# TensorE's signals in the gather stages move from the last matmul to a drain behind it

## The chip, the cores and the metric

One Trainium2 chip, of which the program uses one core. The metric is the device time of one execution in microseconds; lower is better. The engines are TensorE (PE: matmuls, and PEld: its weight loads), VectorE (DVE), ScalarE (ACT), GpSimd (POOL) and SyncE (SP). Each runs its own stream of instructions, and they wait for each other on semaphores.

## The reference

A graph network of two layers, and a mixture of six small experts behind it, on 12,500 nodes of 256 features and 200,000 edges plus a loop at each node:

```python
def gcn_conv(x, W, b, src, dst, n_nodes):
    ...
    norm = dinv[s] * dinv[d]                      # 1/sqrt(degree) of both ends
    xw = x @ W
    msg = xw[s] * norm[:, None]
    out = jax.ops.segment_sum(msg, d, num_segments=n_nodes)
    return out + b
...
out = jax.nn.relu(batch_norm(gcn_conv(x, W1, b1, ...), gamma1, beta1))
out = batch_norm(gcn_conv(out, W2, b2, ...), gamma2, beta2)
out = jax.nn.relu(out + identity)
...
x = x + gnn(layernorm(x), edges, ...)
x = x + experts(layernorm(x), ...)                # router, the best two of six experts
```

The edges arrive sorted by their target node `dst`. All is float32.

## The kernel before, in words

The kernel scales the rows by the degree first, sums the rows of each node's neighbours, and multiplies by W afterwards. It first builds tables of the edges (windows, indices, degrees), then writes the scaled rows to DRAM (`t_dram[0]`), runs a gather stage for layer 1, writes rows again (`t_dram[1]`), runs a gather stage for layer 2, and ends with the router (rows are scattered to `routed`) and the expert tiles.

A gather stage (`gathers` on GpSimd, `aggregate` on the others) works on `NG` = 208 groups of 1024 edges. A group is `CPG` = 8 gathers of 128 rows of 1 KB:

- GpSimd, line 678, fetches 128 rows of DRAM into one of 32 slots of `spare` with an indirect DMA. There is room for `RING` = 4 groups. Ahead of the first gather of group g it waits for `groups_used` >= g - 3, that is until TensorE has used the group four before it. Its indices come from ScalarE (line 801, `stage_ready`), which waits for `groups_used` too.
- VectorE makes a one-hot matrix for each 128 edges (line 1194, `oh_fast`): which of 128 nodes of a window the edge goes to. For group g + 2 it waits for `groups_used` of group g.
- TensorE, `fast`: eight matmuls of a one-hot tile with a slot (line 1753) sum the group into one PSUM bank. A float32 matmul leaves two records in the trace, so a group has 16. The last one raises `groups_used`. Then `turn_window` transposes the window of the group before it (`turn`, line 1653), the last transpose raising `win_turned`.
- ScalarE, line 810, copies the sums of a group out of PSUM to `win_rows` behind `groups_used`, and raises `win_kept`, for which `turn_window` waits.
- VectorE, line 1205, adds the turned window to `acc` behind `win_turned`, at a position that it reads from a table, and raises `ev_fast`.

Once in eight groups the linear part of a finished chunk of nodes lies between (`lin_begin`, `lin_finish`, line 1775 on TensorE; `scale`, line 1242, and `stats`, line 1248, on VectorE; `add_bias`, line 822, on ScalarE); `scale` raises `lin_scaled`. When all groups are added, VectorE raises `agg_done` (line 1266) and the last chunks of the linear part follow. Loops over the groups are hardware loops (`strides`), and the order on each engine is that of the program text.

Behind the second gather stage GpSimd makes masks for the router (lines 695 to 713) once `agg_done` is 2; VectorE reads them behind `masks_made` (lines 1361 to 1365). The masks lie in `spare` and `tables`.

Of the kernel before, what the change touches and what calls it, by code (L numbers as in the profile page):

```python
# [17 lines left out]
P = 128  # L18
# [4 lines left out]
CPG = 8  # L23
GE = EC * CPG
WIN = 128
# [52 lines left out]
def gnn_moe(nc, N, E, x, src, dst, W1, b1, W2, b2, gamma1, beta1, gamma2, beta2,  # L78
            rw1, rb1, rw2, rb2, ew1, eb1, ew2, eb2, ew3, eb3, out):
    D = x.shape[1]  # L80
    KH = D // P
    NX = ew1.shape[0]
    NCH, NG, NT, STRIDE = sizes(N, E)
# [45 lines left out]
    with ExitStack() as ctx:  # L129
# [42 lines left out]
        win_rows = sb("win_rows", [WIN, 2, D])  # L172
        ps = ctx.enter_context(nc.psum_tensor("ps", [P, 8, 512], F32))
# [36 lines left out]
        slots = spare[:, 0:SLOTS * D].rearrange("p (s f) -> p s f", s=SLOTS)  # L210
        onehot_mem = spare[:, SLOTS * D:SLOTS * D + CPG * GWIN]
        onehot = onehot_mem.rearrange("p (u j w) -> p u j w", u=2, j=CPG)
# [129 lines left out]
        stage_ready, groups_used = sem("stage_ready"), sem("groups_used")  # L342
        oh_fast, ev_fast = sem("oh_fast"), sem("ev_fast")
        win_kept, win_turned = sem("win_kept"), sem("win_turned")
# [35 lines left out]
        L1, L2 = 0, 1  # L380
# [269 lines left out]
        def _(pool):  # L650
# [40 lines left out]
            gathers(L2)  # L691


            pool.wait_ge(agg_done, 2)
            pool.iota(iota_pb, pattern=[[RB, B2]], base=0, channel_multiplier=1).then_inc(masks_made, 1)
            pool.memset(tri_f, 1.0).then_inc(masks_made, 1)
            pool.memset(up_to, 1.0).then_inc(masks_made, 1)
# [952 lines left out]
        def _(pe):  # L1650
            def turn(out, in_, last_sem=None):
                n = in_.shape[0]
                return pe.transpose(out, in_, ident[0:n, 0:n])  # L1653
# [74 lines left out]
            def aggregate(run):  # L1728
# [11 lines left out]
                def turn_window(g, u):  # L1740
                    pe.wait_ge(win_kept, g + 1 + run * NG)
                    wait(pe, ev_fast, g - 1 + run * NG if not isinstance(g, int) or g > 1 else 0)
                    hold(pe)
                    for k in range(KH):
                        last = turn(ps[:, 2 + u, k * WIN:(k + 1) * WIN], win_rows[:, u, k * P:(k + 1) * P])
                    last.then_inc(win_turned, 1)

                def fast(i, q):
                    g, u = i * RING + q, q % 2
                    pe.wait_ge(oh_fast, g + 1 + run * (NG + 2))  # L1750
                    for j in range(CPG):
                        landed(q * CPG + j, i)
                        last = pe.matmul(ps[0:WIN, u, 0:D], onehot[:, u, j, 0:WIN], slots[:, q * CPG + j, :],  # L1753
                                         start=j == 0, stop=j == CPG - 1)
                    last.then_inc(groups_used, 1)
                    if not isinstance(g, int) or g > 0:
                        turn_window(g - 1, 1 - u)

# [266 lines left out]
```

## Time and profile before

| | us |
|---|---|
| median of 3 runs | 6157.68 (6153.87 to 6157.74) |
| the profiled execution | 6128.32, span 6126.5 |
| granted TensorE clock, mean | 0.733 of full speed |
| gather stage, layer 1 | 2394.1 |
| gather stage, layer 2 | 2398.0 |
| router and experts, from 5116.1 on | 1010.4 |

The profile comes from one execution. A record is one instruction on an engine; waits on semaphores are not busy time. "Idle before <-releaser" is the time in which the engine had nothing in work ahead of an instruction, and whose signal ended it: "issue" means that the profile shows nothing that was waited for, "remote" that the releaser is not known to it. The ends of matmuls are modelled. Times in the timeline are microseconds from the start of the span.

### The profile page before, as it was taken

The numbers are of one execution on the slowest core, as the hardware profiler recorded it, in microseconds if no ns is written. First come the engines' busy times: TensorE is split into PE (matmuls) and PEld (weight loads), VectorE is DVE, ScalarE is ACT, GpSimd is POOL, SyncE is SP. The second block draws the span as 40 slices with busy tenths as digits, with TensorE's granted clock in tenths as the row PEclk, the third lists the DMA queues.
The fourth block names the chain that finished last, engine by engine and source line by source line (L and its number), as shares of the span: only waits on it lengthen the run. The fifth ranks groups of instructions, "written<-read, shape, count | busy, mean of one in ns | idle before, by whom it ended". The sixth has DMA issues, their size and how long they took to land.

```text
span 6126.5 us, 61161 instructions
## 1 busy us (share of the span) xinstructions
PE 3312.6 (54%) x14297; PEld 2581.7 (42%) x14298; DVE 1868.4 (30%) x6698; ACT 956.1 (16%) x2217; POOL 3417.0 (56%) x3639
## 2 busy tenths in 40 slices
PE   4544544444454444544444445545444445679999
PEld 4433333333333333333333333333333334468888
DVE  8311212121121211141121211212121226657776
ACT  5100000000000000030000000000000004545555
POOL 0466666666666666636666666666666663321111
PEclk5677667767677676776767677667677777779999
DMA  3633333333333333353333333333333333321111
GB/s 113 196 92 95 91 96 91 95 93 92 97 94 92 94 97 93 94 173 88 96 93 92 94 95 92 93 95 92 94 95 93 93 94 89 115 89 49 50 49 46
DMA packets 265334, 577.43 MB, mean 94 GB/s; under 512 B 67455, under 2 KB 140130, under 8 KB 264994
## 3 DMA queue, kind: packets, MB, share of 16 engines
q0 software_dynamic: 171168, 466.40, 26.3%
q1 hardware_dynamic: 92930, 107.84, 6.1%
q10 hardware_dynamic: 1152, 2.20, 0.1%
q8 instruction: 37, 0.61, 0.0%
q14 instruction: 47, 0.39, 0.0%
HBM read 516.09 MB, written 60.09 MB: 94 GB/s over the span
## 4 chain that ended last, share of the span: by engine, by line
another core or an unknown queue 43%; PE 20%; issue 17%; DVE 8%; DVEq 4%; POOL 4%; ACT 2%; DMA 1%; ACTq 0%; SPq 0%; POOLq 0%
PE ps L1960 7%; DVE spare L1194 5%; PE ps L1753 5%; POOL spare L678 4%; PE ps L1975 4%; DVEq L1202 2%; PE ps L1653 2%; DVEq L1194 2%; PE ps L1879 1%; PE ps L1681 1%; PE ps L1775 1%; DMA rows_mem<-in_x_dram 1%; DVEq L55 0%; ACT acc L858 0%
## 5 line engine op out<-in xcount | busy, mean ns | idle before, releaser
L678 POOL DMA_INDIRECT spare<-messages,idx_stage x3328 | 3176.1, 954 | 1791.9 <-issue 1187.2
L1753 PE MATMUL ps<-spare 128*128 128x256 f32 x6656 | 1941.1, 451 | 776.1 <-DVE spare L1194 363.6
L1753 PEld LDWEIGHTS ps<-spare 128*128 128x128 f32 x6656 | 1502.1, 231 | 1174.6 <-issue 524.0
L1205 DVE TENSOR_TENSOR acc<-acc,ps 128x256 f32 x416 | 175.2, 421 | 3821.3 <-remote 3001.3
L1653 PE MATMUL ps<-ident,win_rows 128*128 128x128 f32 x832 | 203.8, 335 | 1762.1 <-DVE acc L1205 1055.3
L1653 PEld LDWEIGHTS ps<-ident,win_rows 128*128 128x128 f32 x832 | 119.0, 166 | 1876.9 <-issue 1852.5
L810 ACT ACTIVATE win_rows<-ps 128x256 f32<-128x256 f32 x416 | 153.9, 383 | 4596.8 <-remote 3598.1
L1194 DVE TENSOR_SCALAR spare<-iota_bf,tables 128x128 f32<-128x128 bf16 x3360 | 718.6, 301 | 51.3 <-issue 45.3
L1960 PE MATMUL ps<-acc 128*128 128x256 f32 x2016 | 459.6, 380 | 0.8 <-ACT acc L988 0.8
L736 POOL DMA_INDIRECT out_dram<-acc x126 | 125.9, 999 | 578.8 <-DVE acc L1603 399.0
L1960 PEld LDWEIGHTS ps<-acc 128*128 128x128 f32 x2016 | 378.9, 190 | 53.2 <-issue 1.2
L1775 PE MATMUL ps<-acc,wconv 128*128 (+1 forms) x448 | 248.2, 693 | 9.3 <-issue 9.3
L1975 PE MATMUL ps<-acc 128*128 128x256 f32 x1008 | 228.2, 379 | 0.0
L1975 PEld LDWEIGHTS ps<-acc 128*128 128x128 f32 x1008 | 190.8, 189 | 27.1
L1552 DVE TENSOR_SCALAR acc<-ps,acc 128x256 f32<-128x256 f32 x252 | 121.7, 483 | 120.9 <-PE ps L1960 81.9
L998 ACT ACTIVATE acc<-ps,acc 128x256 f32<-128x256 f32 x252 | 117.6, 467 | 213.5 <-PE ps L1960 196.5
L974 ACT ACTIVATE acc<-acc 128x1029 f32 x126 | 133.9, 1063 | 65.4 <-issue 61.9
L1775 PEld LDWEIGHTS ps<-acc,wconv 128*128 128x128 f32 x448 | 98.7, 242 | 75.7 <-issue 74.7
L1653 PE MATMUL ps<-ident,acc 128*128 128x128 f32 (+1 forms) x527 | 81.9, 299 | 69.6 <-DVE acc L1333 26.8
L1603 DVE SCALAR_TENSOR_TENSOR acc<-ps,acc 128x256 f32<-128x256 f32 x252 | 110.4, 480 | 12.4 <-PE ps L1975 4.2
L1603 DVE SCALAR_TENSOR_TENSOR acc<-acc 128x256 f32<-128x256 f32 x252 | 110.7, 481 | 6.5
L1653 PEld LDWEIGHTS ps<-ident,acc 128*128 128x128 f32 (+1 forms) x527 | 68.5, 150 | 82.6 <-issue 40.2
(264 smaller groups left out, 2041.1 us busy)
## 6 DMA issues: line engine op xcount, KB each, us to landing
spare<-messages,idx_stage POOLq DMA_INDIRECT x3328
rows_mem<-in_x_dram SPq DMA_DIRECT2D x54, 448.0 KB, 3.9
acc<-routed_rows SPq DMA_DIRECT2D x63, 268.0 KB
spare<-dinv_row SPq DMA_DIRECT2D x56, 224.0 KB, 4.2
messages<-spare SPq DMA_DIRECT2D x23, 448.0 KB, 5.9
spare<-in_x_dram SPq DMA_DIRECT2D x22, 448.0 KB, 4.4
messages<-ring SPq DMA_DIRECT2D x19, 448.0 KB, 4.0
messages<-rows_mem SPq DMA_DIRECT2D x14, 448.0 KB, 3.9
```

Of the source, the lines that this page charges most:

```text
L678: pool.indirect_dma_start(out=slots[:, c % SLOTS, :], out_offset=None, in_=t_dram[layer], in_offset=bass.IndirectOffsetOnAxis(ap=idx_stage ...
L736: pool.indirect_dma_start(out=out, out_offset=bass.IndirectOffsetOnAxis(ap=out_idx[:, u, b:b + 1], axis=0), in_=yrow[u][:, b, :], in_offse ...
L810: act.activation(win_rows[:, u, :], ps[0:WIN, u, 0:D], ACT.Copy).then_inc(win_kept, 1)
L974: act.activation(we[u][x][:, 0:EA].unsqueeze(1), wx[:, bass.ds(e, 1), 0:EA], ACT.Copy).then_inc(expert_a, 1)
L1194: last = dve.tensor_scalar(onehot[:, u, j, :], iota_bf[:, 0:WIN], relT[:, bass.ds(g * CPG + j, 1)], None, ALU.is_equal)
L1205: dve.tensor_tensor(sums(w, WIN), sums(w, WIN), ps[:, 2 + u, 0:KH * WIN].rearrange("p (k w) -> p k w", k=KH), ALU.add).then_inc(ev_fast, 1)
L1603: last = dve.scalar_tensor_tensor(out=yrow[u][:, b, :], in0=terms[b], scalar=wsel[:, u, x, b:b + 1], in1=into[b], op0=ALU.mult, op1=ALU.add)
L1653: return pe.transpose(out, in_, ident[0:n, 0:n])
L1753: last = pe.matmul(ps[0:WIN, u, 0:D], onehot[:, u, j, 0:WIN], slots[:, q * CPG + j, :], start=j == 0, stop=j == CPG - 1)
L1775: last = pe.matmul(ps[:, bank + m, 0:CH], wconv[:, run, k, m * P:(m + 1) * P], acc[:, k, bass.ds(t * CH, CH)], start=k == 0, stop=k == KH - 1)
L1960: last = pe.matmul(ps[:, 1 + 2 * x + m, 0:TOK], w_of(u, x, layer, k, m * P, (m + 1) * P), rhs[:, k, :], start=k == 0, stop=k == KH - 1)
L1975: last = pe.matmul(ps[:, 5 + x, b * D:(b + 1) * D], h2T[x][:, k, b * P:(b + 1) * P], w_of(u, x, 2, k, 0, D), start=k == 0, stop=k == KH - 1)
```

## The change

On TensorE, in `fast` and in `turn_window`, the signals `groups_used` and `win_turned` no longer stand on the last matmul but on a drain instruction that is queued behind it. The drain is meant to wait until these matmuls have finished, and what is queued behind it waits for the drain. On GpSimd the wait ahead of the router's masks is for the last `lin_scaled` of layer 2 (28 chunks) instead of the second `agg_done`.

```diff
@@ -691,7 +691,7 @@
             gathers(L2)
 
 
-            pool.wait_ge(agg_done, 2)
+            pool.wait_ge(lin_scaled[L2], NCH)
             pool.iota(iota_pb, pattern=[[RB, B2]], base=0, channel_multiplier=1).then_inc(masks_made, 1)
@@ -1742,17 +1742,17 @@
                     for k in range(KH):
-                        last = turn(ps[:, 2 + u, k * WIN:(k + 1) * WIN], win_rows[:, u, k * P:(k + 1) * P])
-                    last.then_inc(win_turned, 1)
+                        turn(ps[:, 2 + u, k * WIN:(k + 1) * WIN], win_rows[:, u, k * P:(k + 1) * P])
+                    pe.drain().then_inc(win_turned, 1)
 
                 def fast(i, q):
                     g, u = i * RING + q, q % 2
                     pe.wait_ge(oh_fast, g + 1 + run * (NG + 2))
                     for j in range(CPG):
                         landed(q * CPG + j, i)
-                        last = pe.matmul(ps[0:WIN, u, 0:D], onehot[:, u, j, 0:WIN], slots[:, q * CPG + j, :],
-                                         start=j == 0, stop=j == CPG - 1)
-                    last.then_inc(groups_used, 1)
+                        pe.matmul(ps[0:WIN, u, 0:D], onehot[:, u, j, 0:WIN], slots[:, q * CPG + j, :],
+                                  start=j == 0, stop=j == CPG - 1)
+                    pe.drain().then_inc(groups_used, 1)
                     if not isinstance(g, int) or g > 0:
                         turn_window(g - 1, 1 - u)
```

## Rows read from the trace of the kernel before

**Rows 1.** The page, part 1: busy us (share of the span) xinstructions.
```profile
PE 3312.6 (54%) x14297; PEld 2581.7 (42%) x14298; DVE 1868.4 (30%) x6698; ACT 956.1 (16%) x2217; POOL 3417.0 (56%) x3639
```
**Rows 2.** Busy time by stage: both gather stages, then the router and its tail.
```profile
core 0: us, PE busy (x) PEld busy (x) DVE busy (x) ACT busy (x) POOL busy (x), PEclk, DMA share, GB/s
213.60:2607.70 2394.10, 1126.65 (x3912) 844.72 (x3912) 469.62 (x1920) 112.84 (x356) 1588.68 (x1664) 0.70 0.33 94
...
2699.30:5097.30 2398.00, 1140.30 (x3932) 850.82 (x3933) 472.67 (x1929) 113.26 (x359) 1587.39 (x1664) 0.70 0.32 93
```
**Rows 3.** The page, part 5: busy us, mean ns | idle before it <-releaser.
```profile
L678 POOL DMA_INDIRECT spare<-messages,idx_stage x3328 | 3176.1, 954 | 1791.9 <-issue 1187.2
```
**Rows 4.** Waits of GpSimd in gather stage 1, then 2: us, times, longest us.
```profile
POOL spare L678 <- issue: 587.5, 1585, 84.3
POOL spare L678 <- remote: 267.0, 65, 6.0
POOL spare L678 <- PE ps L1753: 35.2, 14, 5.9
...
POOL spare L678 <- issue: 599.7, 1588, 91.6
POOL spare L678 <- remote: 281.9, 67, 6.0
POOL spare L678 <- PE ps L1753: 20.6, 9, 5.9
```
**Rows 5.** Timeline around one stall: start us, us, instruction [idle before <-releaser].
```profile
2391.57 3.62 PE L1753 MATMUL ps<-spare 128*128 128x256 f32 x16
...
2396.75 2.97 PE L1753 MATMUL ps<-spare 128*128 128x256 f32 x13
...
2404.39 0.58 PE L1753 MATMUL ps<-spare 128*128 128x256 f32 x1 [1.72 <-issue]
...
2410.85 0.95 POOL L678 DMA_INDIRECT spare<-messages,idx_stage  x1 [0.31 <-issue]
2415.71 0.38 ACT L810 ACTIVATE win_rows<-ps 128x256 f32<-128x256 f32 x1 [23.47 <-remote]
...
2416.21 0.38 ACT L810 ACTIVATE win_rows<-ps 128x256 f32<-128x256 f32 x1
...
2416.39 1.02 POOL L678 DMA_INDIRECT spare<-messages,idx_stage  x1 [4.59 <-remote]
```
**Rows 6.** Timeline of the three groups behind that stall.
```profile
2417.82 5.25 PE L1753 MATMUL ps<-spare 128*128 128x256 f32 x16 [0.82 <-DVE spare L1194]
...
2423.12 3.62 PE L1753 MATMUL ps<-spare 128*128 128x256 f32 x16
2423.19 0.38 ACT L810 ACTIVATE win_rows<-ps 128x256 f32<-128x256 f32 x1 [6.59 <-issue]
...
2426.80 3.62 PE L1753 MATMUL ps<-spare 128*128 128x256 f32 x16
...
2442.65 0.38 ACT L810 ACTIVATE win_rows<-ps 128x256 f32<-128x256 f32 x1 [18.97 <-remote]
```
**Rows 7.** Timeline behind the last gather of layer 1.
```profile
2621.06 3.62 PE L1753 MATMUL ps<-spare 128*128 128x256 f32 x16
...
2624.79 0.39 ACT L810 ACTIVATE win_rows<-ps 128x256 f32<-128x256 f32 x1 [3.29 <-PE ps L1753]
```
**Rows 8.** Timeline of the ends of both layers: markers, masks, last scaling, first reader.
```profile
2627.41 0.06 DVE L1266 MEMSET marker<- 128x1 f32 x1
...
5105.75 0.06 DVE L1266 MEMSET marker<- 128x1 f32 x1
...
5109.03 0.10 POOL L712 MEMSET spare<- 128x1 f32 x1
5109.56 1.09 DVE L1242 TENSOR_TENSOR rows_mem<-ps,spare 128x896 f32<-128x896 f32 x1 [0.86 <-issue]
...
5116.31 0.20 DVE L1362 CAST spare<-tables 112x112 bf16<-112x112 f32 x1
```

## The prediction

> **What bounds the kernel now.** I read the busy shares first: no engine is full, GpSimd has 56% and TensorE 54% of the span [rows 1]. The windows by stage then show where the time is: the two gather stages take 2394.1 and 2398.0 us, 78% of the span, TensorE is busy for less than half of each, and GpSimd for 1588.68 and 1587.39 us with 1664 gathers each [rows 2]. So GpSimd's stream of gathers sets the length of these stages, and the question is what interrupts it. One gather takes 0.954 us [rows 3], and the next starts 0.30 us behind it [rows 5]: a pitch of 1.254 us, 1664 x 1.254 = 2086.7 us for a layer. The stages are 307.4 and 311.3 us longer than that, 618.7 us together.
>
> The waits of GpSimd say where these are [rows 4]. In the first layer it stood 267.0 us in 65 waits whose releaser the profile does not know ("remote") and 35.2 us in 14 on the last matmul of line 1753; in the second 281.9 us in 67 and 20.6 us in 9. The one wait inside the stream that another engine can lengthen so is `groups_used`. Together they are 604.7 us in 155 waits; 155 x 0.30 = 46.5 us of it would pass there anyway, so 558 us are stalls. (The "issue" rows hold, beside one wait of 84.3 and one of 91.6 us ahead of each layer, just the 0.30 us between gathers and some 40 us more.)
>
> Next I looked at the timeline around one stall to see whether the matmuls are late or their signal is [rows 5]. The group that begins at 2391.57 ends at 2395.19. The next one follows, 13 records in 2.97 us, and the last record starts at 2404.39 and ends at 2404.97. ScalarE, which waits for nothing but `groups_used` to copy the window, starts at 2415.71, 20.5 us behind the end of the first of them; GpSimd finished its gather at 2411.80, stood until then, and started at 2416.39. TensorE did nothing from 2404.97 on. The matmuls were not late by their records. The signal was.
>
> It is not always so. In [rows 6] the group of 2417.82 is signalled at once (16 records to 2423.07, ScalarE starts at 2423.19), the one of 2423.12 ends at 2426.74 and ScalarE starts at 2442.65, 15.9 us later, though TensorE already runs the group behind it (2426.80 to 2430.42). Behind the last gather of a layer the signal comes at once again: 16 records from 2621.06, ended at 2624.68, ScalarE at 2624.79 [rows 7]. So the delay belongs to the time in which gathers run, it starts with the second group behind each stall, and it ends when GpSimd has stood for 4.6 us (2411.80 to 2416.39). A second sign is the pace inside [rows 5]: 13 records follow each other at 0.23 us, then the last three take until 2404.97. TensorE seems to have a limited number of matmuls that have started and are not yet reported as finished, and to have reached it.
>
> **The change, part by part.** *The signal of a used group* moves from the eighth matmul to a drain behind it, 208 times a layer. Three engines wait for it: GpSimd (the slot is free), ScalarE (copy of the window, next indices) and VectorE (next one-hot tiles). *The signal of transposed sums* moves in the same way, 208 times a layer, with VectorE waiting. No row of before shows such a drain under load, so I bound it from both sides. Cheapest: it is reported when the array is really empty, a fraction of a us behind the matmul, which is what [rows 7] show for a prompt signal (0.11 us). Dearest: it waits for the same late report, some 16 to 20 us [rows 5, 6].
>
> In the cheap case its own price is hidden. What is queued behind a drain on TensorE is the transposes of the window before, the linear part and the next group. A group took 5.25 us from a cold start and 3.62 us warm [rows 6, 7], and GpSimd needs 8 x 1.254 = 10.03 us to fetch one; two drains of a few tenths, with the refill of the array, stay inside the 4.8 us that are left. That cover is gone only behind the last gather of a layer, where three groups are worked off: 3 x 2 x 0.3 = about 2 us a layer.
>
> *What goes.* If the signals become prompt, the ring of 4 groups gives GpSimd 30 us of air between a landed group and its next use, and nothing in the rows is as late as that. All 558 us of stalls go. The end of the first layer gains too: from its last gather (2607.70) to the marker of line 1266 (2627.41) it is 19.7 us, in the second layer, whose last signals happened to be prompt, 8.5 us (5097.30 to 5105.75) [rows 2, 8]. That is another 11 us. Off this go about 4 us for drains behind the last gathers. What is late next is GpSimd itself, at 1.254 us a gather, and nothing below it can be had by signals: the ceiling of the gain is 618.7 + 11 = 630 us.
>
> *GpSimd's wait* ahead of the masks moves from `agg_done` (5105.75) to the last scaling of the linear part, line 1242, which ends at 5109.56 + 1.09 = 5110.65. The masks took until 5109.13, 3.4 us behind their wait, so they end at about 5114.0. The first reader is VectorE's copy at 5116.31 [rows 8]. Cost nothing, with 2.3 us of air; queued behind the masks on GpSimd are only the scatters of the router, which need VectorE's addresses later still. Without that air it would be at most 4.9 us, once.
>
> Sum, in the cheap case: 558 + 11 - 4 = 565 us off. The profiled execution had a span of 6126.5 us in 6128.3; the median of the runs is 6157.7, 0.5% more, and I take the same amount off it: **5593 us**. The bounds of that case are 6157.7 - 630 = 5528 and, if one stall in three stays, 5593 + 558/3 = 5779.
>
> **The rule against it.** The rows show a matmul whose record ends at 2430.42 and a drain would stand right there. The Trainium skill, "PSUM — Partial Sum Buffer", section "Engine vs sequencer instructions", says that an increment on a matmul fires when the matmul completes, and that a drain waits until the engine is fully idle. Read strictly, a drain can then never signal before the matmul would have, and the change can only cost; that is the first rival. The trace neither confirms nor refutes it: it shows late signals, not what a drain makes of them. The Trainium skill, "Perfetto Trace Analysis", section "Tensor Engine Instruction (MATMUL, LD_WEIGHTS)", adds that the end of a matmul in a profile is estimated and that its signal is pushed when PSUM has acknowledged the writes; so a record's end does not prove that all was done. What the rows show for the drain is that after 4.6 us of standing all signals come within a fraction of a us of each other (copies at 2415.71 and 2416.21 for two groups whose records end 9.8 us apart): the work was long done, only its report was held.
>
> **Rivals.** *First, the drain waits for the same late report (slower).* Then TensorE loses its run-ahead, and a stall frees one group, not two as in [rows 5]. With R the moment of release: GpSimd restarts at R + 0.7 and fetches two groups, until R + 20.5, because the group behind the released one is prompt (signal at R + 7.5, [rows 5, 6]: 2415.71 to 2423.19). It then needs the second group behind it, whose report takes 19.5 us from its start (2423.12 to 2442.65), so R + 27; it stands, and a standing of 4.6 us releases it first, at R + 25.1. Two groups in 2 x 10.03 + 4.6 - 0.3 = 24.4 us are 12.2 us a group; 416 x 12.2 = 5075 us against 4792 now [rows 2], 283 us more: 6440 us, and up to 6750 if part of the groups stall one by one. It decides from the point at which a drain is as late as the matmul. For it: the rule above, and the limited number of unreported matmuls. Against it: reports that come in a burst.
>
> *Second, the drain is as late as the matmul but the run-ahead was worth nothing (no change).* The stall pattern stays, 6158 within some 10 us. It needs the releases to fall on the same times although only one group is in flight; I give it little.
>
> *Third, only part becomes prompt.* The lateness begins when TensorE has run for a while beside gathers; a drain that empties the queue each time may only postpone it, so that GpSimd stalls less often. One half of the stalls left gives 5593 + 279 = 5870 us.
>
> *Fourth, TensorE becomes the bound.* With queues emptied twice a group and its clock at the lower level it would have to exceed 10.03 us a group; at half the granted clock a group would need twice the 3.62 us of [rows 7], the transposes 0.7 and the drains under 1: 9 us at most. It doesn't.
>
> **How the numbers follow.** Prompt signals 0.42 (5530 to 5780), partly prompt 0.12 (to 6145), no change 0.08, slower 0.38 (6170 to 6750, most of it around 6440). The likeliest is the first: 5593 us. As both signs hold much of the chance, the range spans them: 5540 to 6600 leaves out a few in 100 below and about 12 above. What a measurement can tell from no change is 0.2%, 12 us.
>
> **What would show it.** Right: GpSimd's "remote" waits in the gather stages fall from 549 us to a few tens, the stages shorten to about 2095 us each, ScalarE's copy of a window starts within a us of the eighth matmul, the pitch of gathers stays 1.254 us. First rival: the same waits or more, TensorE never starts a group before the copy of the one before it, stages above 2500 us. Masks: the first GpSimd record behind the gathers moves behind line 1242 of VectorE, and line 1362 doesn't move with it. I am wrong in size if the pitch of the gathers changes, and wrong in kind if the lateness turns out to be real work of TensorE.

## The result and the profile after

The changed kernel is slower: 6250.59 us median of 4 runs (6250.47 to 6251.06) against 6157.71 us of the kernel before beside it (4 runs, 6153.87 to 6159.34). The ratio is 1.015, with a 95% interval of 1.0137 to 1.0163. The profiled execution has a span of 6248.8 us, 122.3 us more than before.

The page of the kernel after, part 1 and part 5 (busy us, mean ns | idle before it <-releaser), which answer to [rows 1] and [rows 3]:

```profile
PE 3421.2 (55%) x14297; PEld 2602.4 (42%) x14298; DVE 1867.6 (30%) x6698; ACT 963.4 (15%) x2217; POOL 3402.2 (54%) x3639
...
L678 POOL DMA_INDIRECT spare<-messages,idx_stage x3328 | 3160.3, 950 | 1910.1 <-issue 1164.0
...
L1205 DVE TENSOR_TENSOR acc<-acc,ps 128x256 f32 x416 | 175.5, 422 | 3939.0 <-PEq L1746 3343.6
...
L810 ACT ACTIVATE win_rows<-ps 128x256 f32<-128x256 f32 x416 | 159.5, 383 | 4701.8 <-PEq L1755 3951.8
```

A gather costs what it did (950 ns against 954), there are as many of them, and GpSimd stands 118 us longer ahead of them (1910.1 against 1791.9). Who is waited for has a name now: "PEq L1755" is the drain behind a group, "PEq L1746" the one behind the transposes.

The busy time by stage of the kernel after, from the first gather of a layer to its last, which answers to [rows 2]:

```profile
core 0: us, PE busy (x) PEld busy (x) DVE busy (x) ACT busy (x) POOL busy (x), PEclk, DMA share, GB/s
216.60:2662.70 2446.10, 1179.26 (x3892) 851.37 (x3893) 468.82 (x1920) 116.73 (x356) 1579.50 (x1663) 0.73 0.32 92
2753.00:5199.40 2446.40, 1176.50 (x3879) 851.16 (x3880) 465.64 (x1908) 116.66 (x356) 1578.84 (x1663) 0.73 0.32 92
```

Counted from first to last gather in both kernels, a layer took 2393.1 and 2397.1 us before and takes 2446.1 and 2446.4 us now: 102.3 of the 122.3 us. TensorE's granted clock in the stages is no lower (0.73 against 0.70). Counted from the end of the last gather to the marker of line 1266 it is 17.3 us in layer 1 (19.7 before) and 23.1 us in layer 2 (8.5 before), together 12.2 us more; the remaining 7.8 us lie ahead of the first gather (3.0), in the router (4.6) and between the layers (0.2).

The waits of GpSimd in the two gather stages of the kernel after (us, times, longest us), which answer to [rows 4]:

```profile
POOL spare L678 <- issue: 578.1, 1542, 86.6
POOL spare L678 <- PEq L1755: 375.0, 122, 5.0
...
POOL spare L678 <- issue: 585.9, 1546, 89.4
POOL spare L678 <- PEq L1755: 371.1, 118, 5.2
POOL tables L695 <- DVE rows_mem L1242: 28.5, 1, 28.5
```

604.7 us in 155 waits have become 746.1 us in 240. Take off the 0.30 us that pass ahead of any gather, and the stalls are 746.1 - 72.0 = 674 us against 558. They are shorter and come more often. Before, GpSimd stood over 1 us ahead of the first gather of 62 groups of layer 1 and 63 of layer 2, about one group in three, and each of these stands was on average 4.6 us longer than the usual 0.30. Now it does so ahead of 100 groups in each layer, nearly every second one, and a stand is on average 3.4 us longer than the usual.

TensorE's run-ahead is gone. Of the 415 groups of both layers that have one behind them, 273 were followed by the start of the next group's matmuls before their own sums were copied; in the kernel after none is. The copies themselves are less late than before, counted from the end of the group's last matmul record: 225 of 416 come over 1 us behind it against 280, with a median of 10.6 us against 18.3. The matmuls start that much later instead, and GpSimd stands longer.

The timeline of the kernel after through one such cycle (start us, us, instruction [idle before <-releaser]), which answers to [rows 5] and [rows 6]:

```profile
2401.04 0.95 POOL L678 DMA_INDIRECT spare<-messages,idx_stage  x1 [0.30 <-issue]
2405.21 0.38 ACT L810 ACTIVATE win_rows<-ps 128x256 f32<-128x256 f32 x1 [16.63 <-PEq L1755]
...
2405.89 0.94 POOL L678 DMA_INDIRECT spare<-messages,idx_stage  x1 [3.90 <-PEq L1755]
...
2406.29 5.53 PE L1753 MATMUL ps<-spare 128*128 128x256 f32 x16 [0.32 <-issue]
...
2411.95 0.38 ACT L810 ACTIVATE win_rows<-ps 128x256 f32<-128x256 f32 x1 [6.36 <-PEq L1755]
...
2414.14 3.62 PE L1753 MATMUL ps<-spare 128*128 128x256 f32 x16
...
2424.63 0.95 POOL L678 DMA_INDIRECT spare<-messages,idx_stage  x1 [0.30 <-issue]
...
2428.80 0.38 ACT L810 ACTIVATE win_rows<-ps 128x256 f32<-128x256 f32 x1 [15.25 <-PEq L1755]
...
2429.43 0.94 POOL L678 DMA_INDIRECT spare<-messages,idx_stage  x1 [3.85 <-PEq L1755]
...
2429.92 2.47 PE L1753 MATMUL ps<-spare 128*128 128x256 f32 x5 [0.32 <-issue]
```

The group of 2406.29 ends at 2411.82 and is reported at once (2411.95). The group of 2414.14 ends at 2417.76, and its drain reports at 2428.80, 11.0 us later, when GpSimd has stood since 2425.58. In that time TensorE starts nothing, though landed groups lie there: its next group starts at 2429.92. The cycle is 2429.43 - 2405.89 = 23.54 us for two groups, 11.77 us a group. This is the first rival of the prediction, link by link.

### The profile page after: what moved, and what is told of

The parts are those of the page before. It is cut to its first block, busy times and chain, and to the rows that moved or that the text cites. A ratio compares the mean times of both kernels' runs of the same rounds, so it can differ in the third digit from the quotient of the medians.

```text
span 6248.8 us, 61993 instructions
## 1 busy us (share of the span) xinstructions
PE 3421.2 (55%) x14297; PEld 2602.4 (42%) x14298; DVE 1867.6 (30%) x6698; ACT 963.4 (15%) x2217; POOL 3402.2 (54%) x3639
## 3 DMA queue, kind: packets, MB, share of 16 engines
q0 software_dynamic: 171168, 466.40, 25.8%
## 4 chain that ended last, share of the span: by engine, by line
PE 51%; issue 42%; ACT 2%; DVE 2%; DMA 1%; POOL 0%; ACTq 0%; another core or an unknown queue 0%; SPq 0%; DVEq 0%; POOLq 0%
PE ps L1753 30%; PE ps L1960 7%; PE ps L1653 5%; PE ps L1775 4%; PE ps L1975 3%; PE ps L1681 1%; PE ps L1879 1%; DMA rows_mem<-in_x_dram 1%; ACT acc L858 0%; POOL spare L678 0%; ACT spare L890 0%; ACT tables L923 0%; ACT rows_mem L907 0%; ACT ring L915 0%; ACT z_mem L915 0%
## 5 line engine op out<-in xcount | busy, mean ns | idle before, releaser
L678 POOL DMA_INDIRECT spare<-messages,idx_stage x3328 | 3160.3, 950 | 1910.1 <-issue 1164.0
L1753 PEld LDWEIGHTS ps<-spare 128*128 128x128 f32 x6656 | 1529.3, 235 | 629.9 <-issue 354.5
L1653 PE MATMUL ps<-ident,win_rows 128*128 128x128 f32 x832 | 224.4, 363 | 2284.9 <-issue 2284.9
L1653 PEld LDWEIGHTS ps<-ident,win_rows 128*128 128x128 f32 x832 | 102.9, 173 | 2440.5 <-issue 2440.5
L1775 PE MATMUL ps<-acc,wconv 128*128 (+1 forms) x448 | 263.2, 727 | 54.2 <-issue 50.5
```

The costliest lines, as they stand in the source:

```text
L678: pool.indirect_dma_start(out=slots[:, c % SLOTS, :], out_offset=None, in_=t_dram[layer], in_offset=bass.IndirectOffsetOnAxis(ap=idx_stage ...
L1775: last = pe.matmul(ps[:, bank + m, 0:CH], wconv[:, run, k, m * P:(m + 1) * P], acc[:, k, bass.ds(t * CH, CH)], start=k == 0, stop=k == KH - 1)
```

## Experiments

The questions were, in this order: which of the two drains costs the time, and whether the moved wait has a part in it; what it is that holds TensorE's reports; and whether a drain is cheap where nothing holds them. The runs did not all fall on the same chip, and this turned out to decide more than any edit. On one chip, at two times, the kernel before took 6125.48 us (median of 13 runs) and 6160.81 us (1 run), with the stalls of [rows 4 to 6]. On three others it took 5459.01, 5456.99 (13 runs each) and 5449.22 us (1 run), with none. I call them the late and the prompt chips below. Which chip the kernel before and the kernel after of the section above ran on isn't on record; by their times and stalls it was of the late kind. Comparisons are with the kernel before on the same chip at the same time, where nothing else is said.

**One drain at a time, and the masks alone.** group_drain_only is the kernel after with the signal of the transposes on its matmul again, turn_drain_only with that of the group on its matmul again, late_masks_only is the kernel before with GpSimd's wait moved.

```diff
 group_drain_only, in turn_window:
-                    pe.drain().then_inc(win_turned, 1)
+                    last.then_inc(win_turned, 1)
 turn_drain_only, in fast:
-                    pe.drain().then_inc(groups_used, 1)
+                    last.then_inc(groups_used, 1)
```

> The change without its second drain: only the signal of a used group stands on a drain, the signal of the transposed sums is on the last transpose again (GpSimd's later wait ahead of the masks is kept). Theory A (the drain of a group waits for the same late report as the matmul did, and by waiting keeps TensorE from running ahead): nearly all of the loss is here, 6235 to 6255 us, with about 120 stalls of GpSimd a layer as in the changed kernel. Rival B (the two drains each cost a refill of the array, in proportion to their number): half of the loss, about 6205 us.

> Only the signal of the transposed sums stands on a drain; the one of a used group is on the last matmul again. Theory A: this drain stands behind the matmuls of the group too, so it also waits for their late report, and TensorE cannot start the next group before it: the same loss, 6230 to 6255 us, though GpSimd's signal itself is on the matmul. Rival B: half of the loss, about 6205 us. A third reading (only the signal that GpSimd waits for matters): 6158 us.

> Only GpSimd's wait ahead of the masks is moved, no drain. Both theories: 6158 us within 0.2%, the masks end ahead of their first reader by some 2 us.

Measured on the late chip: 6171.91 us, ratio 1.0071 (1.0054 to 1.0088); 6167.89 us, ratio 1.0067 (1.005 to 1.0084); 6124.09 us, ratio 0.9999 (0.9988 to 1.001). So the moved wait costs nothing, and each drain costs by itself 0.7%, about half of what both cost together. It doesn't matter which signal stands on the drain. This is what rival B forecast (half of the loss, 47 us; measured 46 and 42), and my own theory A, nearly all of the loss with either drain, missed. B's reason, a fixed price for each drain on the path, is ruled out further down only where GpSimd's stream covers it: both drains cost 6 us on a chip with prompt signals. That the drains' own price comes onto the path behind a stall of the late chip isn't ruled out. What theory A has wrong is the size: with one drain the run-ahead is already gone (no group starts before the copy of the one before it, in either kernel), and that costs only half. In the medians of the layers the next group's matmuls start 0.4 to 0.6 us behind the copy with one drain and 1.1 to 1.2 us behind it with two, and with two the drain behind the transposes ends over 0.3 us behind their last record in 56 of 416 groups, 113 us together. That may be the other half; no run isolates it. The waits of GpSimd in group_drain_only and in turn_drain_only (whole execution):

```profile
POOL spare L678 <- PEq L1755: 694.1, 251, 5.0
...
POOL spare L678 <- remote: 631.2, 184, 5.0
```

With one drain there are 87 and 94 (group_drain_only), 80 and 84 (turn_drain_only) groups in a layer ahead of which GpSimd stands over 1 us, between the 62 of before and the 100 with both drains. In turn_drain_only the group's signal stands where it stood before and is late all the same (255 of 416 copies over 1 us behind the last record), and TensorE starts the next group only when the transposes in between are reported:

```profile
2406.74 0.39 ACT L810 ACTIVATE win_rows<-ps 128x256 f32<-128x256 f32 x1 [15.61 <-PEq L1746]
...
2406.99 5.79 PE L1753 MATMUL ps<-spare 128*128 128x256 f32 x16 [11.95 <-issue]
2407.42 0.95 POOL L678 DMA_INDIRECT spare<-messages,idx_stage  x1 [3.41 <-remote]
```

That is the price of either drain in these stages: what is queued behind it begins when the held report has come. Here TensorE had nothing in work for 11.95 us.

**Is it work of TensorE, or of its operands?** static_rows takes the matmul's moving operand from the weights (its sums are not those of the reference), so TensorE reads no slot into which a gather writes. one_pass_matmuls has the matmuls read the high 16 bits of both tiles as bf16 (coarser sums), half_the_matmuls leaves out every second matmul of a group.

```diff
 static_rows:
-                        last = pe.matmul(ps[0:WIN, u, 0:D], onehot[:, u, j, 0:WIN], slots[:, q * CPG + j, :],
+                        last = pe.matmul(ps[0:WIN, u, 0:D], onehot[:, u, j, 0:WIN], wconv[:, run, 0, :],
 one_pass_matmuls:
+                        last = pe.matmul(ps[0:WIN, u, 0:D], high_half(onehot[:, u, j, 0:WIN]), high_half(slots[:, q * CPG + j, :]),
 half_the_matmuls:
+                        if j % 2:
+                            continue
```

> The kernel before, but the eight matmuls of a group read one constant tile (the weights) as their moving operand in place of the gathered rows; all waits stay, the sums are wrong. Theory C (the matmuls are really slow, because they read the slots while gathers write beside them): signals become prompt, GpSimd's stalls of 605 us fall to under 100, about 5600 us. Theory A (the report is held whatever is read): unchanged, 6120 to 6180 us.

> The kernel before, but the eight matmuls read only the high 16 bits of both operands as bfloat16, which cuts the messages to bfloat16; one pass and one record a matmul in place of two longer ones. Theory A1: eight short records a group are reported in less than 10 us, the stalls go, about 5600 us. Theory A2: above 6000 us.

> The kernel before with four of the eight matmuls of a group (half of the edges are left out, the sums are wrong); all gathers stay. Theory A1 (each record waits its own turn to be reported, so a group costs about 16 x 1.2 us): the late time halves to below GpSimd's 10.03 us a group, under 100 us of stalls are left, about 5600 us. Theory A2 (the report is held for a time that doesn't depend on the number of records): stalls stay above 400 us, about 6000 to 6130 us.

static_rows, on the late chip, took 6130.46 us (one run) beside 6125.48 and kept its stalls (558.6 us "remote" in 140 waits), so reading beside the gathers' writes is not the cause. The other two ran on a prompt chip, where the kernel before took 5459.01 us and had no stall to lose: 5459.73 us, ratio 1.0001 (0.9991 to 1.0011), and 5456.18 us. They say nothing of the cause, but something else: with stalls gone, TensorE's work may be cut by half and the time doesn't move, so GpSimd's pitch is the bound there.

**Is it the gathers' bytes, or who issues them?** short_rows is static_rows with gathers of 64 bytes a row in place of 1 KB. In plain_rows_by_syncE SyncE's queue fetches 128 consecutive rows into each slot, with the same waits, and GpSimd loads the degree rows that SyncE did; no indirect gather is left in the two stages, and the sums are those of other rows.

```diff
 short_rows:
-                            out=slots[:, c % SLOTS, :], out_offset=None, in_=t_dram[layer],
+                            out=slots[:, c % SLOTS, 0:16], out_offset=None, in_=t_dram[layer].rearrange("n (a f) -> (n a) f", f=16),
 plain_rows_by_syncE:
+                        sp.dma_start(slots[:, c % SLOTS, :], t_dram[layer][c * P:(c + 1) * P, :]).then_inc(got[c % SLOTS // QUAD], 16)
```

> The kernel before with its gathers replaced: SyncE fetches 128 consecutive rows of 1 KB for each slot through its hardware queue, with the same waits; GpSimd only loads the degree rows. The rows are not those of the edges, so the sums are wrong. Theory A (matmuls are reported late because of GpSimd's descriptor work): every group is signalled within 0.5 us of its last matmul, the gather stages fall to what TensorE needs, 5 to 7 us a group, 1000 to 1500 us a layer, in all 4000 to 4700 us. Theory D (they are late because of DMA traffic into SBUF of any kind): the lateness stays or grows with twice the traffic, signals 10 us and more late.

> The kernel with a constant moving operand (6130 us), and gathers that move 64 B a row in place of 1 KB, with the same number of descriptors; the sums are wrong. Theory A (GpSimd's descriptor work): unchanged, 6080 to 6180 us, some 65 stalls a layer. Theory D (bytes on their way into SBUF): the stalls go, about 5600 us.

These ran on the prompt chip too: 3006.25 and 5450.9 us beside 5459.01. The first is far under the 4000 to 4700 us that were expected, and says how much GpSimd's pitch costs (nearly half of the whole time); neither says anything of a delay that wasn't there.

**The chip.** The kernel before and the kernel after were run again unchanged, and two of the last ones once more, for a chance of the other kind.

> The kernel before, unchanged, for its own trace beside the others of this chip: in one comparison it took 6125 us, in the next, on another chip, 5459 us. Theory E (the reports of matmuls are late on some chips only): either about 6130 us with some 125 stalls of GpSimd in both layers, or about 5460 us with no stall above 1 us and the copy of each window within 0.2 us of the eighth matmul; nothing between. Theory F (the lateness comes and goes within one chip from run to run): times between, or a spread of over 100 us among the runs of the kernel before.

> The changed kernel. Theory A (a drain costs only because it waits for a late report and keeps TensorE from running ahead): 1.5% slower where the kernel before takes 6130 us, and within 0.1% where it takes 5460 us, since GpSimd's 10 us a group cover two prompt drains. Rival B (each drain costs a fixed refill on the path): slower by the same 95 us or so in both cases.

> Constant moving operand and gathers of 64 B a row, again; it has sense only where the kernel before takes 6130 us. Theory A (descriptor work of GpSimd is what makes reports late): 6080 to 6180 us. Theory D (bytes on their way): about 5600 us or less. Where the kernel before takes 5460 us: 5450 us as before.

> Four of eight matmuls a group (half of the edges left out), again, for a chip on which the kernel before takes 6130 us. Theory A1 (each record waits its own turn to be reported): 5450 to 5600 us. Theory A2 (the report is held for a time of its own): 5900 to 6130 us.

It was another prompt chip. The kernel before took 5445.82 us in that execution (median of the 13 runs 5456.99), the kernel after 5463.08 us, ratio 1.0011 (1.0002 to 1.0021), short rows 5446.96, half of the matmuls 5452.78. The timeline of before_again and, behind the dots, of after_again:

```profile
2402.93 3.03 PE L1753 MATMUL ps<-spare 128*128 128x256 f32 x8 [3.00 <-DMA spare<-messages,idx_stage]
...
2406.05 0.38 ACT L810 ACTIVATE win_rows<-ps 128x256 f32<-128x256 f32 x1 [8.86 <-PE ps L1753]
2406.34 0.21 ACT L801 ACTIVATE idx_stage<-tables 128x16 int32<-128x16 int32 x1
2406.35 0.95 POOL L678 DMA_INDIRECT spare<-messages,idx_stage  x1 [0.31 <-issue]
...
2405.96 3.53 PE L1753 MATMUL ps<-spare 128*128 128x256 f32 x8 [2.46 <-DMA spare<-messages,idx_stage]
...
2409.61 0.38 ACT L810 ACTIVATE win_rows<-ps 128x256 f32<-128x256 f32 x1 [11.20 <-PEq L1755]
2409.76 0.41 PE L1653 MATMUL ps<-ident,win_rows 128*128 128x128 f32 x2 [0.27 <-issue]
```

In before_again the matmuls end at 2405.96 and the copy starts at 2406.05; TensorE waits for landing rows, not for reports. In after_again they end at 2409.49, and the copy starts at 2409.61. Each of the 416 drains behind a group ends 0.02 us behind the last matmul's record. From first to last gather a layer took 2083.8 and 2085.5 us in before_again (1664 x 1.251 = 2081.7), with no gap over 1 us. The copy of a group's sums comes at most 0.2 us behind its last record in all 416 groups, in both kernels.

The same program thus takes 12% more time on the late chip, and nine tenths of the difference lie in the two gather stages. What is left is what holds the reports there. The next runs fell on the late chip again:

> Constant moving operand and gathers of 64 B a row, for a chip on which the kernel before takes some 6130 us. There: theory A (GpSimd's descriptor work, or the semaphore steps that every gather ends with, whatever it moves) 6080 to 6180 us; theory D (bytes on their way) about 5600 us or less. On a chip where the kernel before takes 5460 us: 5450 us, which tells nothing.

> SyncE fetches consecutive rows for each slot, GpSimd does nothing in the gather stages. Where the kernel before takes some 6130 us: theory A in its narrow form (GpSimd's descriptor work) 3010 us as on the other kind of chip; theory H (the 16 semaphore steps of each landing transfer crowd out TensorE's reports) well above it, 4000 us or more, since the steps come twice as fast. Where it takes 5460 us: 3010 us, which tells nothing.

> Four of eight matmuls a group (half of the edges left out). Where the kernel before takes some 6130 us: theory A1 (each record waits its own turn to be reported) 5450 to 5650 us; theory A2 (the report is held for a time that doesn't depend on the number of records) 5900 to 6130 us. Where it takes 5460 us: 5455 us, which tells nothing.

Beside 6160.81 us, short_rows_3 took 6159.95 (GpSimd stands over 1 us ahead of 67 and 72 groups), half_matmuls_3 6115.11 (53 and 59), plain_rows_3 3062.05, one run each. The waits of GpSimd in the first two and the timeline of plain_rows_3:

```profile
POOL spare L678 <- remote: 597.5, 134, 6.3
...
POOL spare L678 <- remote: 547.4, 111, 8.4
```

```profile
703.60 3.62 PE L1753 MATMUL ps<-spare 128*128 128x256 f32 x16
707.05 0.38 PE L1653 MATMUL ps<-ident,win_rows 128*128 128x128 f32 x2
707.27 3.62 PE L1753 MATMUL ps<-spare 128*128 128x256 f32 x16
707.38 0.38 ACT L810 ACTIVATE win_rows<-ps 128x256 f32<-128x256 f32 x1 [4.74 <-PE ps L1753]
707.57 0.42 DVE L1205 TENSOR_TENSOR acc<-acc,ps 128x256 f32 x1 [3.19 <-PE ps L1653]
710.73 0.38 PE L1653 MATMUL ps<-ident,win_rows 128*128 128x128 f32 x2
710.94 3.62 PE L1753 MATMUL ps<-spare 128*128 128x256 f32 x16
711.01 0.38 ACT L810 ACTIVATE win_rows<-ps 128x256 f32<-128x256 f32 x1 [3.24 <-PE ps L1753]
```

Nothing is late here, on the chip where two of three groups are late otherwise: the group that ends at 710.89 is copied at 711.01, and every copy of a window is within 0.2 us of its eighth matmul. The DMA engines move as many bytes into the same slots, more than twice as fast, and the same semaphores count them. With a sixteenth of the bytes per row and gathers issued by GpSimd the reports are as late as ever (300 of 416 copies over 1 us behind their group's last record, against 280 in the kernel before). With half of the matmuls they are as late too (296 of 416), and only the stalls are somewhat fewer. So the volume of traffic into SBUF, landing transfers as such and the number of matmuls are out; the lateness goes with the indirect gathers.

Which part of an indirect gather it is, isn't shown. plain_rows_3 takes away GpSimd's work for it, the software-driven DMA queue that it feeds (171,168 packets in the kernel before, 15,008 here) and the scattered source rows, all at once. It also changes TensorE's own state: in the plain gather stages TensorE is nearly always busy, at a granted clock of 0.97, where it stands for more than half of the time in the kernel before, at 0.70. On a prompt chip (before_again) it stands for 39% of the gather stages at a clock of 0.80 and nothing is late, so standing alone doesn't do it; whether it has a part on the late chip wasn't tried.

**Does a pause of GpSimd let a report through?** The stalls of before end when GpSimd has stood for some 4 us. But that isn't the only way out: of the 280 late copies of the kernel before, 67 came while its stream of gathers ran on, half of them over 10.9 us behind their group's last record. The copy at 2442.65 of [rows 6] is one; the gathers of the kernel before around it:

```profile
2441.59 0.95 POOL L678 DMA_INDIRECT spare<-messages,idx_stage  x1 [0.30 <-issue]
2442.85 0.95 POOL L678 DMA_INDIRECT spare<-messages,idx_stage  x1 [0.31 <-remote]
```

The last kernels put pauses into GpSimd's stream, fills of a buffer that nobody reads, and repeat the one-pass matmuls for the late chip.

```diff
 pause_each_group: three times, behind the wait of each group; pause_each_gather: once, ahead of each gather
+                            pool.drain()
+                            pool.memset(pause_mem[:, :], 0.0)
```

> The kernel before, with three fills of a buffer that nobody reads (128x512 each, a drain of GpSimd ahead of each) in front of the first gather of every group; what is computed stays the same. By the fills in the trace (0.286 us for 128x225) one is about 0.65 us, so each group gets a pause of some 2.0 us in GpSimd's stream of gathers, 416 x 2.0 = 830 us in all. Theory R (a held report gets through whenever GpSimd issues no gather for a moment): on a chip with late reports GpSimd stalls in fewer than 15 places a layer instead of 62, ScalarE's copies of a window follow the eighth matmul within some 3 us, and the time is 6160 - 610 + 830 = 6380 us. Theory T (a pause changes nothing, a report needs its time or a standing of over 4 us): the stalls stay at 50 to 60 a layer and the copies stay up to 30 us late, and the time is about 6160 + 830 = 6990 us. On a chip with prompt reports both give 5457 + 830 = 6290 us and no stalls.

> The kernel before, with one fill of that unread buffer (128x512, a drain of GpSimd ahead of it) in front of every gather; what is computed stays the same. A gather then comes every 1.9 to 2.0 us instead of every 1.254, 3328 x 0.7 = 2330 us more. Theory R (short pauses let the reports through): no stalls over 1 us, copies of a window prompt, and on a chip with late reports 6160 - 610 + 2330 = 7880 us. Theory T (only the standing of over 4 us lets them through): the stalls stay, at least 40 a layer, and the time is 8400 us or more. On a chip with prompt reports both give 5457 + 2330 = 7790 us. If the pauses come out shorter or longer than 0.7 us the times move with them; the number of stalls and the lateness of the copies tell the theories apart.

> The kernel before, with the group's matmuls reading the high 16 bits of their tiles as bf16, so that one pass stands in place of the passes of a 4-byte matmul; the sums are coarser, all else is the same. Theory P (the report is held by work that TensorE itself has still to do): with the matmul's work cut to a fraction the stalls of GpSimd fall to under 30 a layer, and on a chip with late reports the time is under 5900 us. Theory Q (the report is held from outside, however short the matmul): stalls stay at 50 to 70 a layer of about 4.6 us, and the time is within 1% of the kernel before. On a chip with prompt reports both give the time of the kernel before within 0.2%.

They ran on a prompt chip (5449.22 us before): 7086.85, 13237.81 and 5454.17 us, no late report in any. The question stays open. What the runs do show is that my price for the pause was far off, 6290 and 7790 us expected. The timeline of pause_each_gather:

```profile
2001.68 0.52 POOL L680 MEMSET pause_mem<- 128x512 f32 x1 [1.91 <-issue]
2002.38 0.95 POOL L681 DMA_INDIRECT spare<-messages,idx_stage  x1 [0.17 <-issue]
2005.27 0.52 POOL L680 MEMSET pause_mem<- 128x512 f32 x1 [1.94 <-issue]
```

The fill takes 0.52 us, but it starts 1.94 us behind the record of the gather (2003.33 to 2005.27), and gathers come every 3.59 us instead of every 1.25. Without a drain the next gather starts 0.30 us behind that record. The drain alone is short: in pause_each_group, where three fills of 0.52 us with a drain ahead of each stand together, the second and third start 0.64 and 0.65 us behind the one before them (2005.59, 2006.23, 2006.88). So some 1.8 us of work or wait of a gather stand behind its record, and the records of GpSimd show less than what it is at.

## Why the prediction was wrong, point by point

**The reading of the bound was right.** GpSimd's stream bounds the gather stages, and 558 us of its waits were stalls on late reports. The prompt chips show what the change was to bring, as far as chips can be compared: without late reports the unchanged kernel needs 5457 to 5459 us, some 700 us under the 6157.7 of the case's own median. Of the 682.4 us between the spans of before (6126.5) and before_again (5444.1) the two stages make 2393.1 + 2397.1 - 2083.8 - 2085.5 = 620.9 us, as [rows 2] gave (618.7). What the ceiling of 630 us left out is 54.9 us behind the last marker, in the router (1020.7 us against 965.9), where GpSimd issues indirect scatters too; it wasn't traced further.

**The step that failed** is the choice between the ends of the drain's cost, "Cheapest: it is reported when the array is really empty". From it came the term of 558 us of stalls that were to go; 674 us of stalls are there. It was taken with 0.42 against 0.38, on the sign that two groups' signals came within half a microsecond of each other, which was read as: the work was long done, only its report was held. That may be so (no run tells a matmul that really ended late from one that was only reported late, as the ends of matmul records are modelled), and it would not have helped. What a drain waits for is held with the report: the group of 2414.14 above ended at 2417.76 and its drain reported at 2428.80. The drain is held where the matmul was, and it adds that TensorE stands until then. The Trainium skill, "PSUM — Partial Sum Buffer", section "Engine vs sequencer instructions", which the prediction set against its own choice, says that an update on a matmul fires at its completion and that a drain waits until the engine is wholly idle. By that, a drain can't be earlier. On both kinds of chip the drains come behind the group's last record (each 0.02 us behind it on the prompt one; 0.02 to 21.6 us behind it in the kernel after, 11.0 us in the row above). The evidence for the choice bore on why the report was late, not on whether a drain gets past it, and should have moved no chance.

**A reading that was too narrow** lies beside it: the delay "ends when GpSimd has stood for 4.6 us". The prediction's own [rows 6] hold a late report that came while gathers ran on, and 67 of the 280 late ones did.

**The first rival was right in each link and too dear in one.** It forecast a restart of GpSimd 0.7 us behind the release (measured 2405.89 - 2405.21 = 0.68), the next group's signal 7.5 us behind it (measured 6.7), then a standing that releases the second group, two groups a cycle. It took the standing of before, 4.6 us, and a cycle of 24.4 us; the standings are 3.8 us on average (3.85 in the row), 3.4 above the usual 0.30, and the cycle is 23.54 us. 100 of them in a layer instead of 104 make 2446 us a layer, against 2537 forecast. With the measured terms the sum is 208 x 10.03 + 100 x 3.4 + some 20 us of shorter gaps, and 6251 us came out instead of 6440. The term that was mis-sized is the length of the standing, carried over from the kernel before. There two groups were held at the moment of release [rows 5], not one; that this is why it was longer was not shown.

**The range held the time and the sign was wrong.** The range reached to 6600 on account of this rival, so that it held the time is no merit of the forecast of 5593. The rival's own range, from 6170, held the time too.

**No change** (second rival): the run-ahead was worth something, 1.5%. **Partly prompt** (third): half of its condition came. The late copies fell from 280 to 225 of 416 and their median from 18.3 to 10.6 us, but the stalls rose, because the matmuls that are reported sooner also start later. In the rows shown the group behind a stall is reported promptly in both kernels, and the second one is late in both. **TensorE the bound** (fourth): not so, the groups take 3.62 to 5.53 us of 11.77; on the prompt chip, where it would matter most, both drains cost 6 us in 5457.

**The masks** behaved as worked out. The timeline of the kernel after, which answers to [rows 8]:

```profile
5223.46 0.06 DVE L1266 MEMSET marker<- 128x1 f32 x1
...
5227.76 1.09 DVE L1242 TENSOR_TENSOR rows_mem<-ps,spare 128x896 f32<-128x896 f32 x1 [0.86 <-issue]
...
5228.94 0.14 POOL L695 IOTA tables<- 128x8 int32 x1 [28.54 <-DVE rows_mem L1242]
...
5232.08 0.10 POOL L712 MEMSET spare<- 128x1 f32 x1
5234.51 0.20 DVE L1362 CAST spare<-tables 112x112 bf16<-112x112 f32 x1
```

They end at 5232.18, 2.3 us ahead of their reader, the air that was forecast, and late_masks_only puts the cost at 0.9999 (0.9988 to 1.001).

**The drains' own price behind the last gathers** was put at 2 us a layer. The copies there follow each other at 4.56 us (2664.03 to 2677.72 in three steps), where a group behind the last gather took 3.67 us before (2621.12 to 2624.79 [rows 7]): 3 x 0.9 = 2.7 us a layer, near enough. The copies of before, and behind the dots of after:

```profile
2621.12 0.38 ACT L810 ACTIVATE win_rows<-ps 128x256 f32<-128x256 f32 x1 [8.87 <-PE ps L1753]
...
2664.03 0.38 ACT L810 ACTIVATE win_rows<-ps 128x256 f32<-128x256 f32 x1 [9.22 <-PEq L1755]
...
2677.72 0.38 ACT L810 ACTIVATE win_rows<-ps 128x256 f32<-128x256 f32 x1 [4.18 <-PEq L1755]
```

What the sum hadn't is the length of layer 2's end, 23.1 us against 8.5: at its last gather three groups had not been begun, where in the kernel before only the last one had not. That short end of before was luck, as the prediction says, and without its run-ahead TensorE doesn't have it.

## What stays open

Why one chip holds TensorE's reports while indirect gathers run, and three others don't, isn't settled. The runs show what has to be going on for it, not which part of a gather does it nor the place where the report waits. All these figures come from recorded executions, and the traces of the late kind lack most of their semaphore records; whether the recording itself has a part in the lateness wasn't tried. Whether a deliberate pause of GpSimd would let reports through isn't known, since those kernels ran on a prompt chip only. One-pass matmuls were not seen on the late chip. And why a second drain costs as much as the first, when the first already takes the run-ahead, is not isolated.

## What to carry to other kernels

A drain gets no signal past a held report: it is held with the matmul that it stands behind, and then also holds back everything queued behind it. Here it cost next to nothing where reports were prompt (0.1% for 832 drains) and 0.7% for each 416 where they were late. When a signal is late by the records, first ask what else is running (here, by leaving the indirect gathers out), and run the kernel on a second chip before the lateness is taken for a property of the program. And evidence on why something is late isn't evidence that another instruction gets past it: price the change by what the new instruction itself waits for.

## What the runs showed of the hardware that I had not expected

- The same program took 6125 to 6161 us on one chip and 5449 to 5459 us on three others (medians or single runs); between two traces, 620.9 of 682.4 us of the difference are gather stages, with late reports of TensorE beside GpSimd's indirect gathers. In the first trace of the kernel before, the copy of a window starts over 1 us behind the last record of its group in 67% of the 416 groups, at most 32 us.
- The traces of the late kind hold fewer changes of semaphores: 22,539 in before and 24,302 in after, against 68,595 in before_again on a prompt chip; plain_rows_3, on the late chip and with nothing late, has 66,970. With it releasers are "remote" in [rows 4] that have a name in before_again. Whether the lost records and the late reports have one cause was not tried.
- A group of plain rows was fetched by SyncE's queue and used in 3.7 us (707.27 to 710.94), while a group of gathers takes GpSimd 10.03 us: 3062.05 against 6160.81 us on the late chip, 3006.25 against 5459.01 us on a prompt one, for other rows of the same size.
- What stands behind a drain of GpSimd starts 1.94 us behind the record of an indirect gather, where the next gather would start after 0.30 us; behind a fill the same drain lets the next fill start 0.12 us after its end.
